# Two inputs of the running-maximum step moved from SBUF to PSUM in a two-layer graph network kernel

## What is computed

```
Wd, Ws, ww = Wm[:H], Wm[H:2 * H], Wm[2 * H]
msgs = z[edge_dst] @ Wd + z[edge_src] @ Ws + edge_weight[:, None] * ww[None, :] + bm
agg = segment_max(msgs, edge_dst);  agg = where(deg > 0, agg, 0)
hidden = relu(z @ W1a + agg @ W1b + b1)
return hidden @ W2 + b2
```

## Time and profile before

| | us |
|---|---|
| median of 3 runs | 2271.08 (2266.31 to 2273.05) |
| the profiled execution, device time | 2279.13 |
| its span | 2277.4 |
| granted TensorE clock, mean share of full | 0.881 |
| POOL busy | 1643.7 (72%) |
| TensorE busy | 1658.0 (73%) |
| VectorE busy | 1326.4 (58%) |
| ScalarE busy | 1119.3 (49%) |

### The profile page before, as it was taken

How to read it: one execution, slowest core, us unless ns; L and a number is a source line. 1 busy time by engine, 2 the same in 40 slices (tenths; PEclk the granted TensorE clock), 3 DMA queues, 4 the chain that set the end, 5 groups by cost and what they waited for, 6 DMA issues and landing times. The chain is left out here.

```text
span 2277.4 us, 43250 instructions
## 1 busy us (share of the span) xinstructions
PE 1658.0 (73%) x9891; PEld 1016.1 (45%) x9891; DVE 1326.4 (58%) x5220; ACT 1119.3 (49%) x3305; POOL 1643.7 (72%) x1705
## 2 busy tenths in 40 slices
PE   4687777778777887860767777776777776778774
PEld 4222222222232222210636666665666665667574
DVE  4665555555554444444656656666666666666559
ACT  1243433334434444540556656655565666556548
POOL 3777777777777777775657777777777777777625
PEclk7799999999988999985979988899888889888978
DMA  8634434343433343432432222222222222222214
GB/s 255 205 126 143 130 127 129 125 145 127 144 108 125 128 139 111 144 128 82 128 108 67 65 63 63 66 65 65 66 63 64 65 66 66 60 65 66 65 47 124
DMA packets 115983, 235.04 MB, mean 103 GB/s; under 512 B 32909, under 2 KB 68230, under 8 KB 106422
## 3 DMA queue, kind: packets, MB, share of 16 engines
q0 software_dynamic: 52832, 109.39, 19.9%
q1 hardware_dynamic: 56522, 97.21, 11.6%
q10 hardware_dynamic: 6540, 27.42, 3.4%
HBM read 166.01 MB, written 67.89 MB: 103 GB/s over the span
## 5 line engine op out<-in xcount | busy, mean ns | idle before, releaser
L209 POOL DMA_INDIRECT acc<-d_src_product,b_region x784 | 772.0, 985 | 239.4 <-issue 217.4
L463 POOL DMA_INDIRECT d_region<-d_h,d_region x784 | 758.1, 967 | 248.4 <-issue 216.1
L859 DVE SCALAR_TENSOR_TENSOR acc<-b_region,acc 128x128 f32<-128x128 f32 x784 | 271.7, 347 | 456.4 <-DMA acc<-d_src_product,b_region 456.1
L1577 DVE TENSOR_TENSOR acc<-acc,banks 128x160 f32 x784 | 252.6, 322 | 231.0 <-PE banks L1379 93.0
L651 PE MATMUL banks<-acc,b_region 64*128 64x512 f32 x1176 | 321.9, 655 | 38.3 <-ACT gate_col L756 17.9
L1345 PE MATMUL banks<-shift_ident,d_region 128*128 128x128 f32 x784 | 136.0, 299 | 240.7 <-DMA d_region<-d_h,d_region 231.6
L870 DVE SCALAR_TENSOR_TENSOR acc<-acc,b_region 128x128 f32<-128x128 f32 x784 | 270.2, 345 | 0.2 <-DVE acc L859 0.2
L1376 PE MATMUL banks<-d_region 128*128 128x128 f32 x1568 | 258.4, 319 | 0.0
L1379 PE MATMUL banks<-d_region,pick 128*128 128x128 f32 x1568 | 245.6, 307 | 0.0
L1376 PEld LDWEIGHTS banks<-d_region 128*128 128x128 f32 x1568 | 244.5, 236 | 0.7
L756 ACT ACTIVATE acc<-banks,b_region 128x1024 f32<-128x1024 f32 x147 | 158.8, 1112 | 167.9 <-PE banks L651 167.7
(11 more groups left out here) (261 smaller groups left out, 2394.4 us busy)
## 6 DMA issues: line engine op xcount, KB each, us to landing
d_runs<-acc SPq DMA_DIRECT2D x48, 1024.0 KB, 4.4
acc<-ea ACTq DMA_DIRECT2D x25, 1024.0 KB, 5.5
acc<-d_src_product,b_region POOLq DMA_INDIRECT x784
d_region<-d_h,d_region POOLq DMA_INDIRECT x784
d_region<-d_rel SPq DMA_DIRECT2D x49, 256.0 KB
hT<-xT SPq DMA_DIRECT2D x7, 448.0 KB, 6.9
d_src_product<-acc SPq DMA_DIRECT2D x7, 448.0 KB, 4.5
d_gates<-acc ACTq DMA_DIRECT2D x196, 6.0 KB
```

The lines of the kernel that those rows point to most:

```text
L209: pool.indirect_dma_start(self.rows[:, s, j, :], None, d["B"], bass.IndirectOffsetOnAxis(self.idx[:, k:k + 1], 0)).then_inc(self.gathered[ ...
L463: pool.indirect_dma_start(rows[:, s, :], None, table, bass.IndirectOffsetOnAxis(idx[:, s:s + 1], 0)).then_inc(gathered[q], 16)
L859: nc.vector.scalar_tensor_tensor(rows[:, s, j, :], wwb, wgt[:, k:k + 1], rows[:, s, j, :], ALU.mult, ALU.add).then_inc(ch, 1)
L1577: nc.vector.tensor_tensor(w, w, UZ[q % 2][:, :, j, :], ALU.add).then_inc(ad, 1)
```

## The change

The weights row is copied once into PSUM bank 0, columns 384 to 511 (`wwp`), and three places for a weighted row stand before it in the same bank (`stepped`, STEPS = 3). `step(k)` reads `wwp` from PSUM and the gathered row from SBUF and writes `stepped[k % 3]`; `run(k)` reads `H` from SBUF and that place. The gathered row is not written any more, and its place is free once step is done, so POOL's wait is on the step (`s_done`). As bank 0 is in use for the whole pass, all other work in it moves: the replicated has-edges row of the node part goes to bank 2, the shifted counts and `hidden_out` to bank 1. With bank 2 in use by the replicated row, `node_part(c)` waits for ScalarE's negated hidden rows (`h1c`) where it waited for `gd`.

```diff
+STEPS = 3
...
+        stepped = t["psum"][0][:, 0:STEPS * P].rearrange("p (s f) -> p s f", f=P)
+        wwp = t["psum"][0][:, STEPS * P:(STEPS + 1) * P]
...
+        def s_done(k):
+            return 2 * k if k else 1
...
                 if g >= RG:
-                    pool.wait_ge(ch, r_done(4 * (g - RG) + 3))
+                    pool.wait_ge(ch, s_done(GJ * (g - RG) + GJ - 1))
...
             def hidden_out(c):
-                    last = nc.tensor.matmul(bank[0][:, k * P:(k + 1) * P], negH1[:, c * G4 + k * P:c * G4 + (k + 1) * P],
+                    last = nc.tensor.matmul(bank[1][:, k * P:(k + 1) * P], negH1[:, c * G4 + k * P:c * G4 + (k + 1) * P],
...
             def shifted_counts():
-                view = bank[0][:, 0:2 * NBLK].rearrange("p (a b) -> p a b", a=2)
+                view = bank[1][:, 0:2 * NBLK].rearrange("p (a b) -> p a b", a=2)
...
             def node_part(c):
                     pe.wait_ge(h2d, c)
-                    pe.wait_ge(gd, c)
+                    pe.wait_ge(h1c, c)
                 for k in range(z):
-                    nc.tensor.matmul(bank[0][:, k * P:(k + 1) * P],
+                    nc.tensor.matmul(bank[2][:, k * P:(k + 1) * P],
...
-                    nc.scalar.activation(hrep[:, 0:n], bank[0][:, 0:n], ACT.Copy).then_inc(hrc, 1)
+                    nc.scalar.activation(hrep[:, 0:n], bank[2][:, 0:n], ACT.Copy).then_inc(hrc, 1)
...
             c.link(nc.vector.tensor_tensor(bf, bank[1][:, 0:M], b1, ALU.add))
+            c.link(nc.vector.tensor_copy(wwp, wwb))
...
-                nc.vector.scalar_tensor_tensor(rows[:, s, j, :], wwb, wgt[:, k:k + 1], rows[:, s, j, :],
+                nc.vector.scalar_tensor_tensor(stepped[:, k % STEPS, :], wwp, wgt[:, k:k + 1], rows[:, s, j, :],
                                                ALU.mult, ALU.add).then_inc(ch, 1)
...
-                nc.vector.scalar_tensor_tensor(H[:, k % n, :], H[:, (k - 1) % n, :], rst[:, k:k + 1], rows[:, s, j, :],
-                                               ALU.add, ALU.max).then_inc(ch, 1)
+                nc.vector.scalar_tensor_tensor(H[:, k % n, :], H[:, (k - 1) % n, :], rst[:, k:k + 1],
+                                               stepped[:, k % STEPS, :], ALU.add, ALU.max).then_inc(ch, 1)
```

More of the change, by code:

```diff
@@ L686, in shifted_counts @@
                 pe.wait_ge(cnt, NBLK)
-                view = bank[0][:, 0:2 * NBLK].rearrange("p (a b) -> p a b", a=2)
+                view = bank[1][:, 0:2 * NBLK].rearrange("p (a b) -> p a b", a=2)
                 nc.tensor.matmul(view, t["shift"], cp, start=True, stop=True)
-                nc.tensor.matmul(bank[0][0:1, 2 * NBLK:4 * NBLK], ident[:, P - 1:P], cp, start=True, stop=True
+                nc.tensor.matmul(bank[1][0:1, 2 * NBLK:4 * NBLK], ident[:, P - 1:P], cp, start=True, stop=True
                                  ).then_inc(has, 1)
@@ L858, in step @@
                     dve.wait_ge(gat[s], 64 * (k // (GJ * RG) + 1))
-                nc.vector.scalar_tensor_tensor(rows[:, s, j, :], wwb, wgt[:, k:k + 1], rows[:, s, j, :],
+                nc.vector.scalar_tensor_tensor(stepped[:, k % STEPS, :], wwp, wgt[:, k:k + 1], rows[:, s, j, :],
                                                ALU.mult, ALU.add).then_inc(ch, 1)
             def run(k):
-                s, j = k // GJ % RG, k % GJ
                 if k % ST16 == 0 and k >= HB * ST16:
@@ L893, in has_edges @@
                 c.link(nc.vector.scalar_tensor_tensor(total, cp[:, 0, :], float(EP), cp[:, 1, :], ALU.mult, ALU.add))
-                turned = bank[0][:, 0:4 * NBLK].rearrange("p (n a b) -> p n a b", n=2, a=2)
+                turned = bank[1][:, 0:4 * NBLK].rearrange("p (n a b) -> p n a b", n=2, a=2)
                 c.link(nc.vector.tensor_copy(cp, turned[:, 0, :, :]))
@@ L926, in less_hidden @@
                 v = xb[:, 4 * k:4 * k + z, :]
-                nc.vector.tensor_tensor(v, v, blocks_view(bank[0], 0, z), ALU.subtract).then_inc(h2d, 1)
+                nc.vector.tensor_tensor(v, v, blocks_view(bank[1], 0, z), ALU.subtract).then_inc(h2d, 1)
             step(0)
```

## The result

The changed kernel takes 2246.19 us in the median of four runs (2244.24 to 2249.16), against 2272.07 us before: a ratio of 0.9888, 95% interval 0.9870 to 0.9905. It is 25.9 us faster. I had forecast 2256 us and a range from 2247 to 2268. The span of the profiled execution is 2244.8 us.

The account below looks back on a forecast made before the run. POOL's back-to-back gathers were taken to bound the first pass. Freed gathers, -15.1 us, plus 0 to +0.5 for the rest, call it -15, from the 2271.08 us median gave 2256 us, range 2247 to 2268.

Parts of the forecast that it names:

- POOL bounds the first pass and has no slack: First pass: lasts as long as POOL's 784 gathers; POOL waits for nobody, resting only a fixed 0.3 us between them.
- Steps and runs with one SBUF tensor free 261 delayed gathers, -15.1 us: First pass: 261 gathers beginning beside a step or run each lose 0.058 us; one SBUF input removes that, -15.1 us.
- The step's price: VectorE's step with PSUM operands: taken as nothing, at most 0.13 us more each, hidden except 0.5 us in the last group.
- Rival 5: First pass: VectorE becomes the bound because a step reads and writes one bank; 2290 us, chance 0.02.
- rival 2: First pass: only one of step and run is freed, about half the gain, -7.5 us, 2264 us; chance 0.04.
- The copy, the release, the banks at nothing: Weights-row copy (under 0.35 us, hidden), POOL's release by the step, and node part in banks 1 and 2: no cost.
- it waits for transfers, as I read it: First pass: a gather taking 3.39 us, 10 us after a 1 MB feature load's issue, was read as waiting for transfers.
- rivals 3 and 4: First pass: 3, eight more stalls eat the gain, 2268 us, 0.05; 4, 23 loads each stall a gather, 2309 us, 0.03.
- the lower end of the range: 2247 us: all 16.3 us above the gathers' floor and half of the stalls' 14.9 us gained.
- the prediction's doubt of a full block: First-pass gathers: blocking until the instruction's end would sum to an estimated 45 us, above the 16.3 held, so 0.058 each stood.

Follow-up runs that it names:

- each half of the change: Changed kernel with only the weights row in PSUM: 2252.01 us, ratio 0.9922; with only the weighted rows in PSUM: 2251.72 us, ratio 0.9914.
- Cut the rows alone: Kernel before, plus a VectorE memset of a 128-column scratch tile after every second run, SBUF reads unchanged: 2262.58 us, ratio 0.9949.
- the second profile of the kernel before: The kernel before, unchanged, measured and profiled once more: 2275.27 us, ratio 1.0013.

## Why the prediction was right and where it was wrong

- *POOL bounds the first pass and has no slack:* right. Its waits are the fixed gap before and after, and 30.2 us less in the gathers moved the last gather by 29.1 us.
- *Steps and runs with one SBUF tensor free 261 delayed gathers, -15.1 us:* right. 6 gathers between 0.97 and 1.2 us are left of 193, the small delays fell by 16.6 us over a fixed floor, of which 1.7 are the floor's own shift, and each half of the change frees the gathers beside its own instruction.
- *The step's price:* right. Steps take 354 ns (347 before), runs 337 (345); a step that reads and writes one bank has not the 0.13 us that I set as the upper end. Rival 5 falls with it (its own sum, 2256 + 27, is 2283 us and not 2290), and rival 2 with the gathers freed beside both instructions.
- *The copy, the release, the banks at nothing:* right; banks alone 1.0010, release undone 0.9864 against 0.9888, the two intervals overlapping.
- *"it waits for transfers, as I read it":* **the step that failed.** From it the ten stalls' 14.9 us were left out of the sum and appeared only as something that might grow (rivals 3 and 4) or, half of it, as the lower end of the range. The runs put in its place: a stall is a gather kept out by an unbroken row of two-input instructions. Cut the rows alone, and 11.3 us are gained. The term for the stalls, put at nothing, measures -13.6, by the two profiles. With it the sum is -15.1 - 13.6 = -28.7 on the profiled execution, whose last gather moved by 29.1; the medians moved by 25.9.
- The evidence was in the trace of before. The row of the longest stall, 64.87 us, stands in the first long row of steps, and a check of VectorE at each stall's end, like the one made for the small delays at each start, would have shown the same 0.82 us every time. It would also have shown that the prediction's doubt of a full block was misplaced: a delayed gather is held to the instruction's end, and the mean of 0.058 us is small because many of the 261 begin at a point where nothing holds them. I left the stalls out of that table because they were long, and explained them by the nearest load.

## What to carry to other kernels

When GpSimd issues indirect DMAs one after the other and nothing else bounds a stage, look at what VectorE has open as each of them begins and as each long one ends. Every vector instruction with two SBUF tensors can hold a gather that begins beside it to its end, and an unbroken row of them can keep a gather out to its end; an operand moved to PSUM freed the gathers here, and one harmless instruction every microsecond ended the stalls, though not the small delays. Do not leave the outliers of a group to another cause before they have had the same test as the rest.

## What the hardware showed that I had not expected

A gather that has missed its turn can be kept out by back-to-back two-input vector instructions for as long as they last: up to 2.9 us beyond its 0.945, ending 0.81 to 0.83 us after the last instruction or the first break. It is not a strict rule: in the second profile of the kernel before, a gather begun at 803.16 us missed one boundary and got in at the next (1.26 us), in the middle of a row. In the first profile the eight that met a longer row began 0.14 to 0.16 us after a vector instruction's start, while others in that same window got through; what decides between them stays open. (In the second profile the stalls in longer rows began 0.11 to 0.17 us after a start.) A POOL memset of one column lies wholly in the 0.3 us gap between two gathers, where it costs nothing. VectorE wrote and read the same PSUM bank in one instruction at 354 ns, 7 ns more than from SBUF.
